# Aligning both halves of a warped path from its two corners in one Trainium2 kernel

## The reference, cut

```python
D = sqrt(max(aa + bb - 2 * xn @ ctx.T, 0))        # 128 x 128 distances of a batch
R[i, j] = D[i, j] + min(R[i-1, j], R[i, j-1], R[i-1, j-1])
# walk back from (127, 127) to (0, 0): the smallest of diagonal, up, left (the first at a tie)
expanded[j] += small[i]   for every (i, j) on the path
x = x + tanh(g_xattn[3]) * expanded
```

## Time and profile before

| | |
|---|---|
| median of 3 runs | 1556.9 us (1552.32, 1556.9, 1558.84) |
| the profiled execution | 1551.98 us, its span 1550.2 us |
| busy in the span | PE 1349.5 us, DVE 873.2, ACT 769.4, POOL 387.6 |
| the changed part | 1297.8 to 1470.3 us of the span |

### The profile page before, as it was taken

One profiled execution on the slowest core, in us unless ns is written; L12 is line 12 of the kernel. 1 busy time (PEld: TensorE's weight loads), 2 busy tenths in 40 slices (PEclk: granted clock), 3 DMA queues, 4 the chain that ended last, 5 costly groups with the idle time before them and its releaser, 6 DMA issues. The chain is left out here.

```text
span 1550.2 us, 31871 instructions
## 1 busy us (share of the span) xinstructions
PE 1349.5 (87%) x10589; PEld 1134.4 (73%) x10598; DVE 873.2 (56%) x2230; ACT 769.4 (50%) x1908; POOL 387.6 (25%) x544
## 2 busy tenths in 40 slices
PE   8999878889799999988999989999999998210588
PEld 5888646677689998767888869699999996210355
DVE  6988755656412222207777755623232274688887
ACT  5666474520354443537777753355555433340277
POOL 1000000012032221001222121356666544320141
PEclk9999999999899999999999997799999998655799
DMA  7200000772421117554434422022222354321001
GB/s 222 70 20 15 2 28 19 255 264 42 160 80 38 36 32 229 193 193 138 133 130 135 147 49 82 17 76 93 93 93 94 78 197 163 54 19 8 1 14 41
DMA packets 119253, 145.40 MB, mean 94 GB/s; under 512 B 39248, under 2 KB 96352, under 8 KB 119008
## 3 DMA queue, kind: packets, MB, share of 16 engines
q1 hardware_dynamic: 98048, 94.78, 19.4%
q0 software_dynamic: 10848, 27.88, 6.4%
q10 hardware_dynamic: 10240, 21.24, 3.9%
HBM read 105.22 MB, written 37.49 MB: 92 GB/s over the span
## 5 line engine op out<-in xcount | busy, mean ns | idle before, releaser
L3822 PEld LDWEIGHTS L2f_bank<-L2f_xT,L2f_w_tile 128*128 128x128 f32 x1264 | 154.1, 192 | 7.5 <-ACT L2f_xT L3895 3.5
L3822 PE MATMUL L2f_bank<-L2f_xT,L2f_w_tile 128*128 128x128 f32 x1264 | 154.8, 276 | 3.0 <-ACT L2f_xT L3895 3.0
L3959 DVE TENSOR_TENSOR L2f_hT<-L2f_gate_h,L2f_bank 128x256 f32<-128x256 f32 x79 | 33.3, 421 | 148.9 <-ACT L2f_gate_h L3902 148.9
L1188 ACT ACTIVATE L2x_probs<-L2x_shifted,L2x_top 128x128 f32<-128x128 f32 x256 | 99.0, 388 | 20.9 <-DVE L2x_top L1263 20.9
L1055 POOL TENSOR_TENSOR L2x_probs<-L2x_probs,L2x_inv_sum 128x512 f32<-128x512 f32 x32 | 33.3, 1039 | 264.1 <-DVE L2x_inv_sum L1272 264.1
L3745 POOL DMA_INDIRECT L2f_y_rows<-L2f_xn,L2f_put_row x79 | 78.0, 987 | 55.7 <-DVE L2f_xn L3975 52.1
L3889 ACT COPY L2f_w_tile<-L2f_w_up 128x1024 f32 x79 | 82.7, 1046 | 18.2 <-issue 18.2
L3737 POOL DMA_INDIRECT L2f_rows<-L2f_x_rows,L2f_take_row x79 | 76.8, 972 | 44.9 <-DVE L2f_take_row L3706 21.2
L3822 PEld LDWEIGHTS L1f_bank<-L1f_xT,L1f_w_tile 128*128 128x128 f32 x736 | 85.7, 192 | 2.8 <-ACT L1f_hT L924 1.7
L3822 PE MATMUL L1f_bank<-L1f_xT,L1f_w_tile 128*128 128x128 f32 x736 | 86.0, 275 | 1.5 <-ACT L1f_hT L924 1.5
L3839 PE MATMUL L1f_bank<-L1f_w_down,L1f_hT 128*128 x368 | 83.1, 379 | 0.0
(11 more groups left out here) (696 smaller groups left out, 3300.2 us busy)
## 6 DMA issues: line engine op xcount, KB each, us to landing
L1f_w_up<-in_L_ffn_w SPq DMA_DIRECT2D x16, 512.0 KB, 8.3
L1f_w_down<-in_L_ffn_w SPq DMA_DIRECT2D x16, 512.0 KB, 9.2
L2x_kT<-L2x_k_ahead SPq DMA_DIRECT2D x16, 512.0 KB, 4.6
L2x_v<-L2x_v_ahead SPq DMA_DIRECT2D x16, 512.0 KB, 3.3
L2f_got<-L2f_y_rows SPq DMA_DIRECT2D x16, 512.0 KB, 4.4
L2x_k_ahead<-L1f_w_tile ACTq DMA_DIRECT2D x11, 512.0 KB, 2.9
L2x_v_ahead<-L1f_w_tile ACTq DMA_DIRECT2D x11, 512.0 KB, 2.6
L2f_w_up<-in_L_ffn_gate_w SPq DMA_DIRECT2D x16, 256.0 KB, 3.7
```

The costliest lines, as they stand in the source:

```text
L1188: x = nc.scalar.activation(probs[c][:, i, :], shifted[c][:, i, :], ACT.Exp, scale=-1.0, bias=top[:, c, i:i + 1], accum_out=total[:, c, i:i ...
L3822: x = nc.tensor.matmul(products(j, m), w_tile[j][:, at:at + P], xT[j][:, k * P:(k + 1) * P], start=(k == 0), stop=(k == KT - 1))
L3959: nc.vector.tensor_tensor(hT[j][:, 0:F], gate_h[j][:, 0:F], bank[2 + j][:, F:2 * F], ALU.mult).then_inc(q["h"], 1)
```

## The change

The cost table is split at row 64. The first half is walked from the corner (0, 0), the second from (127, 127) with rows and columns reversed, both at once: 2 directions x 16 batches x 4 strips are 128 lanes, and the wave has 64 + 24 = 88 steps. NB falls from 8 to 4, so a block still has R = 16 rows. At the end the path's cell in the two middle rows is the minimum over the sum of the last rows of both halves (the "meeting"), and each half is walked back from there. For the reversal, TensorE multiplies with constants `both_ways` (identity and reversed identity, 256 columns) and `half_turned`, in plain products in place of transposes; the codes are put in order by one more product. The norm of x is computed from variance and rstd instead of from squares.

```diff
-    NB = 8
-    R = P // NB
+    H = P // 2
+    HB = 2 * B
+    NB = 4
+    R = H // NB
-    STEPS = P + (NQ - 1) * LEAD
+    STEPS = H + (NQ - 1) * LEAD
-    LANES = NQ * B
+    LANES = NQ * HB
...
-            eng.dma_start(dist3[q * B:(q + 1) * B, 1:CW, first:first + P], dist_dram[:, q * C:(q + 1) * C, :]
-                          ).then_inc(s[f"placed{q}"], 16)
+            for h in range(2):
+                at = q * HB + h * B
+                eng.dma_start(dist3[at:at + B, 1:CW, first:first + H],
+                              dist_dram[:, q * C:(q + 1) * C, h * H:(h + 1) * H]).then_inc(s[f"placed{q}"], 16)
...
-                sp.dma_start(low3[B:LANES, land, 0:1], cost3[0:LANES - B, edge, C:CW],
+                sp.dma_start(low3[HB:LANES, land, 0:1], cost3[0:LANES - HB, edge, C:CW],
...
+            nc.gpsimd.memset(both_ways[:, :, :], 0.0).then_inc(s["turned"], 1)
+            nc.gpsimd.memset(half_turned[:, :], 0.0).then_inc(s["turned"], 1)
...
-            def squares(b):
-                act.wait_ge(s["xn"], b + 1)
-                after(act, s["x_norm"], b)
-                nc.scalar.activation(x_sq[:, :], xn[b % 3][:, :], ACT.Square, accum_out=cols(x_norm, b, 1)
-                                     ).then_inc(s["x_norm"], 1)
+            def back_half(b):
+                act.wait_ge(s["dots"], b + 1)
+                act.wait_ge(s["x_norm_back"], 2)
+                after(act, s["dist"], b - 1)
+                nc.scalar.activation(sq_dist[b % 2][:, H:P], bank[4 + b % 2][:, H:P], ACT.Relu,
+                                     bias=x_norm[:, 1, b:b + 1]).then_inc(s["sq_back"], 1)
...
             def root(b):
+                back_half(b)
+                act.wait_ge(s["sq_back"], b + 1)
                 act.wait_ge(s["sq_dist"], b + 1)
...
-                    t = nc.tensor.transpose(bank[b % 2][:, k * P:(k + 1) * P], xn[b % 3][:, k * P:(k + 1) * P],
-                                            core.ident[:, :])
+                    t = nc.tensor.matmul(bank[b % 2][:, k * D:(k + 1) * D], xn[b % 3][:, k * P:(k + 1) * P],
+                                         both_ways[:, :, :].rearrange("p h c -> p (h c)"), start=True, stop=True)
...
-                    t = nc.tensor.transpose(bank[2 + b % 2][:, k * P:(k + 1) * P], ctx_all[:, b, k * P:(k + 1) * P],
-                                            core.ident[:, :])
+                    t = nc.tensor.matmul(bank[2 + b % 2][:, k * P:(k + 1) * P], ctx_all[:, b, k * P:(k + 1) * P],
+                                         half_turned[:, :], start=True, stop=True)
...
-                for k in range(KT):
-                    t = nc.tensor.matmul(dst, xT[b % 2][:, k * P:(k + 1) * P], ctx_neg2[b % 3][:, k * P:(k + 1) * P],
-                                         start=False, stop=(k == KT - 1))
+                for h in range(2):
+                    for k in range(KT):
+                        t = nc.tensor.matmul(dst[:, h * H:(h + 1) * H], xT[b % 2][:, k, h, :],
+                                             ctx_neg2[b % 3][:, k * P + h * H:k * P + (h + 1) * H],
+                                             start=False, stop=(h == 1 and k == KT - 1))
...
-            stay_warm(core, bank[7], 3)
+            stay_warm(core, bank[7], 2)
...
             pe.wait_ge(weights.sems["T_out"], 12)
+            pe.wait_ge(s["swap"], 2)
+            pe.wait_ge(c["blocks"], 16 * (NB * NQ + 1))
+            nc.tensor.matmul(bank[6][:, 0:HB], costs3[0:HB, R, 1:W], swap[:, :], start=True, stop=True
+                             ).then_inc(c["met"], 1)
...
+            dve.wait_ge(c["met"], 1)
+            nc.vector.tensor_copy(last_row[:, :], bank[6][:, 0:HB]).then_inc(c["met"], 1)
...
+            for d in range(2):
+                last = nc.vector.tensor_tensor(step_cost[:, d, :], costs3[0:HB, R, 1:W], other[:, d:d + P], ALU.add)
+            link(last)
...
+            link(nc.vector.tensor_reduce(best, step_cost[:, :, :], AX.XY, ALU.min))
+            link(nc.vector.scalar_tensor_tensor(step_cost[:, :, :], step_cost[:, :, :], best, preferred[:, :, :],
+                                                ALU.is_equal, ALU.mult))
+            link(nc.vector.tensor_reduce(chosen, step_cost[:, :, :], AX.XY, ALU.max))
...
+            nc.vector.tensor_copy(placed[:, :], bank[7][:, B:3 * B]).then_inc(c["placed_out"], 1)
```

More of the change, by code:

```diff
@@ L2699, in warped_alignment @@
         part = lambda at, n, k: [scratch[:, at + j * n:at + (j + 1) * n] for j in range(k)]
-        xn, xT, ctx_neg2 = part(0, D, 3), part(3 * D, D, 2), part(5 * D, D, 3)
+        xn, ctx_neg2 = part(0, D, 3), part(5 * D, D, 3)
+        xT = [t.rearrange("p (k h c) -> p k h c", k=KT, h=2) for t in part(8 * D + 2 * D + 3 * P, 2 * D, 2)]
         ctx_sq, ctx_sum = part(8 * D, D, 2), part(10 * D, P, 3)
-        x_sq = sb("x_sq", [P, D])
-        x_norm = sb("x_norm", [P, B])
+        x_norm = sb("x_norm", [P, 2, B])
+        both_ways = sb("both_ways", [P, 2, P])
+        half_turned = sb("half_turned", [P, P])
+        swap = sb("swap", [HB, HB])
         sq_dist = [sb(f"sq_dist{j}", [P, P]) for j in range(2)]
@@ L2712, in warped_alignment @@
             "quarter", "cleared", "xn", "xT", "xT_out", "ctxT", "ctx_neg2", "ctx_sq", "ctx_sum", "x_norm", "dots",
-            "sq_dist", "dist", "low", "row"] + [f"placed{q}" for q in range(NQ)] + [f"hand{i}" for i in range(HANDS)])
+            "sq_dist", "sq_back", "dist", "low", "row", "turned", "x_norm_back", "swap"] + [f"placed{q}" for q in range(NQ)] + [f"hand{i}" for i in range(HANDS)])
         c = core.sems_in("L3c", ["blocks", "step", "iota", "leave", "gathered", "enter", "entry", "ways", "turn", "unit",
-                                 "codes", "placed", "bounds", "signs", "mark", "out", "updated"])
+                                 "met", "codes", "placed", "placed_out", "ordered", "bounds", "signs", "mark", "out", "updated"])
         load_of = [i for i, n in enumerate(LOADS) for _ in range(n)]
@@ L2745, in warped_alignment @@
         inward = sb("inward", [P, P], BF16)
-        entry16 = sb("entry16", [B, NB])
-        spread = sb("spread", [B, NB, B])
-        of_block = sb("of_block", [P, NB])
+        entry16 = sb("entry16", [HB, NB])
+        spread = sb("spread", [HB, NB, HB])
+        of_block = sb("of_block", [P, 2, NB])
+        first_half = sb("first_half", [P, 4])
+        forward = sb("forward", [HB, 4])
+        other = sb("other", [HB, W])
+        step_cost = sb("step_cost", [HB, 2, P])
+        preferred = sb("preferred", [HB, 2, P])
+        meeting = sb("meeting", [HB, 4])
+        last_row = sb("last_row", [P, HB])
         of_batch = sb("of_batch", [P, B])
@@ L2869, in _ @@
             finish_norm_scalar(core, act, s, temps)
-            squares(0)
             take_xT(0)
@@ L2873, in _ @@
                 if b + 1 < B:
-                    squares(b + 1)
                     take_xT(b + 1)
@@ L2960, in _ @@
             pe.wait_ge(c["enter"], 1)
-            nc.tensor.matmul(bank[7][:, 0:1], spread[:, :, :].rearrange("b k c -> b (k c)"), core.ones[0:B, 0:1],
+            nc.tensor.matmul(bank[7][:, 0:1], spread[:, :, :].rearrange("b k c -> b (k c)"), core.ones[0:HB, 0:1],
                              start=True, stop=True).then_inc(c["entry"], 1)
@@ new lines, in _ @@
+            link(last)
+            link(nc.vector.tensor_scalar(preferred[:, 1, :], preferred[:, 1, :], 1.0, None, ALU.add))
+            dve.wait_ge(c["met"], 3)
+            link(nc.vector.tensor_copy(other[:, 0:P], bank[6][0:HB, P:2 * P]))
+            for d in range(2):
+                last = nc.vector.tensor_tensor(step_cost[:, d, :], costs3[0:HB, R, 1:W], other[:, d:d + P], ALU.add)
+            link(last)
+            best, chosen, diagonal = meeting[:, 0:1], meeting[:, 1:2], meeting[:, 2:3]
```

120 lines of the change are left out of this document (86 added, 34 removed).

## The result

In the same series of runs, twenty of each, the kernel before took 1554.76 us (median) and the changed one 1559.34 us. The ratio is 1.0038, with a 95% interval from 1.0026 to 1.0049: 4 to 8 us slower, inside the 0.5% that the prediction put ahead as "no change". By the medians it is +4.6 us, by the ratio +5.9; forecast was +5.6, and a time of 1562.5.

What follows compares the result with a forecast made beforehand. Each stage has its own limit: TensorE for distances, VectorE for wave and walk back. Terms 15.1+0.4+1.7+1.0-12.3-1.5+1.2 = +5.6 us on the median 1556.9 gave 1562.5 us; range 1552 to 1570.

Steps and rivals of the forecast that it cites:

- Distance stage: TensorE's distance products: more passes make a batch 2.42 us instead of 1.10; the stage's end moves by +15.1 us.
- narrow passes are cheap: Rival for the distance product: a pass of 64 columns costs half, saving 7.0 us, -1.4 in all, 1555.5 us; chance 0.12.
- The hand from ScalarE to VectorE: End of the last distance batch: one more half-width instruction and a semaphore lengthen it by +0.4 us.
- Read-back: Distances coming back in eight transfers of 256 B packets instead of four of 512 B: +1.7 us, between 0 and +3.4.
- First edge: First edge transfer of the wave queues on SP's ring behind the read-back; VectorE waits at step 9, 0 to 4, +1.0 us.
- Lanes are free: Wave: going from 64 to 128 lanes adds nothing to a step of 0.490 us.
- A scan longer than 0.23 us: Wave: a scan instruction above this time was listed as a sign that the forecast is wrong.
- Wave, ternary work, meeting: Wave to walk back: 64 fewer steps save 31.4 us, but 13.9 us go waiting for ternary weights; -12.3 us net.
- Joins and order of the marks: After the meeting: four of seven joins between blocks go, -1.5 us; ordering the marks costs +1.2 us.
- Signs: Marking stage: signs with a per-lane scale cost nothing, as ScalarE has 5.6 us to spare, 0.17 for each of 32.
- The norms: Distance stage: the norms cost nothing; 16 squares leave ScalarE, four small VectorE steps join during TensorE's warm-up.

Runs made afterwards that it cites:

- run 5: Kernel before with the distance product in four calls of 64 columns instead of two of 128; distance end +5.9 us, a batch 1.51 us instead of 1.11.
- Run 6: Kernel before with all TensorE distance work as in the changed one, identity twice instead of a reversal; 1566.55 us, ratio 1.0067, distance end +15.6 us.
- Run 8: Kernel before with each read-back transfer split in two of 64 columns, packets of 256 B; 5.42 us from issue to first step against 5.47.
- run 10: Changed kernel with reversal as transposes, scales before step 16, and SP's queue issuing only the first read-back transfer, ScalarE's the other three; 1540.14 us, ratio 0.9927.
- Run 1: Changed kernel with VectorE's two weight-scale instructions before step 16 of the wave instead of step 80; 1547.82 us, ratio 0.995 to the kernel before.
- run 2: Kernel before with VectorE's two weight-scale instructions before step 16 instead of step 80, as control; 1552.59 us, ratio 0.9988.
- run 11: Kernel before with x's norm taken from the norm's constants, no squares on ScalarE; distance end 26.7 us instead of 29.3, 2.0 us inside the part.
- run 7: Kernel before with the wave's tiles over 128 lanes, upper half zero, transfers as they were; wave 77.2 us instead of 74.5.
- run 3: Changed kernel with the reversing products as transposes, one pass instead of two; 1555.12 us, ratio 1.0002 to the kernel before.

## Why the prediction was right, point by point

Each term was measured inside the part, changed kernel against before. In short: the path was right, the longer distance stage and the ternary weights that wait for step 80, and with them the two large terms; of the small ones, read-back and first edge had the wrong reason, and the dearer steps and the signs were put at nothing.

- **Distance stage, forecast +15.1: +15.4.** The batch of 2.42 us came out, and so did the reading of the earlier trace rows that a narrow pass costs as much as a wide one: 0.105 in run 5. So the rival "narrow passes are cheap" is out. The some 60 cycles up to 64 columns in the Trainium skill, "TensorE: Matmul & The Clock Gate", section "Back-to-back issue gap", are the gap of a product alone, and the section itself says that at small widths this counts too little in a stream of weight loads and products. The trace agrees with that: 0.105 us for 64 columns, with a load each. Run 6 shows that passes alone explain the stage.
- **The hand from ScalarE to VectorE, forecast +0.4:** +0.4.
- **Read-back, forecast +1.7, the middle between bytes (0) and count (+3.4): +1.4.** The size was right by luck: other profiles of the two read-backs put it anywhere from +0.2 to +1.5. The middle stood for no cause. Run 8 shows that the count alone costs nothing; in the changed kernel, whose packets took 51 ns, the last transfer lands 3.1 us later than before. The Trainium skill, "DMA: Bandwidth & Descriptors", section "Specifications", puts the smallest transfer at line rate at 512 B. This case doesn't settle it: in run 8 packets of 256 B came in at the time of those of 512, in the changed kernel they did not. What makes the difference, four runs did not find. That no transfer in the rows had smaller pieces was a slip: the earlier trace rows has packets of 4 B.
- **First edge, forecast +1.0: +1.6** (1.6 us at step 9, where the kernel before has no wait). It does stand behind the read-back, but not by way of SP's ring: with one transfer ahead of it there, run 10 still has 1.3 us. In every profile it lands right behind the read-back's last transfer, so this term and the one above seem to have one cause.
- **"Lanes are free": wrong by a little.** Doubling them adds 8 and 11 ns to the two instructions of a step, some 1.7 us over the 88 steps. "A scan longer than 0.23 us" was one of the signs of being wrong, and the scan takes 0.239; the term is small, so the sum held all the same. I had two rows of different widths and read from them a rule that they only bound.
- **Wave, ternary work, meeting, forecast -12.3: -9.7 from the wave's first step to the walk back**, or -11.3 of forecast with the edge's wait in it. The mechanism was right in each part: ScalarE's chain 20.5 us as before, meeting 5.1 against 5.2, and the wait found where it was put. Of the 1.6 us missing 1.5 are the dearer steps ahead of step 80 (79 x 0.019) and 0.6 the longer wait for the first edge; two waits of 0.25 us, which the kernel before has among those steps and this one once, give some of it back. Run 1 took the wait away and 13.75 us came back, where the text had 13.9; run 2 shows that in the kernel before the same line was worth nothing.
- **Joins and order of the marks, forecast -0.3: -0.5** up to the bounds.
- **Signs, forecast 0: +0.4** from the bounds on. An ACTIVATE with a per-lane scale takes 0.50 and 0.48 us instead of 0.41 and 0.39. Two of them per batch are 0.78 us from start to start. But ScalarE is busy 12.6 of 16.3 us, so 3.7 of the 5.6 us to spare are left, and the stage's clock also differs (0.81 against 0.89). That the signs make the 0.4 is not shown.
- **The norms, forecast 0:** at most 0.2 us in the changed kernel, whose distance end is 44.7 against 44.9 in run 6, which keeps the squares. Alone in the kernel before they were worth some 2 us in the one profile of run 11, where the clock did not fall.

The sum was +5.6 forecast, +7.4 in the pair of profiles, +4.6 to +5.9 over twenty runs. The difference of 1.5 to 2.8 us between profile and runs is of the size of what the distance end alone moves between executions with other clocks at their start (27.3 to 29.3 us in run 7 and the kernel before, whose distance stages are the same). That the whole times agree with the forecast to within a microsecond is therefore partly luck; that it is a small loss and not a gain of some 8 us follows from the path that the prediction had right.

## What to carry to other kernels

Shortening the longest stage moves everything that was timed by it. Here a side chain hung on a step number ("step 80") that had been in the middle of a wave and came to lie at its end. When a loop is cut short, look for the work that is released from inside it, and give it an earlier step, if its inputs exist by then: worth 13.75 us here, and nothing before the cut.

In these traces an f32 product with a constant 0/1 matrix takes two passes, the transpose form with the same constant takes one (2.42 and 1.70 us a batch), and the result was right with a permutation in place of the identity. And cutting a product into narrower calls did not cut its time: with 128-wide weights a pass of 64 columns cost what one of 128 did, 0.105 us.

A mean between two bounds can come out right and stand for no cause. Only runs that take away one cause at a time tell whether the middle was knowledge.

## What the runs showed of the hardware

- Doubling the lanes from 64 to 128 cost 184 to 192 ns for a minimum over 32 columns and 228 to 239 ns for a scan over 33 (run 7).
- A read-back in packets of 256 B (run 8) took no longer than one of the same bytes in packets of 512 B (5.42 and 5.47 us to the first step), while equal packets of 256 B in the changed kernel cost 51 ns instead of 34 (open).
- A small transfer that is issued while a large one is under way landed 0.2 to 1.2 us behind the large one's last piece, in all fourteen profiles, also where it was alone on its queue (run 10: 4.5 us instead of the usual 1.8).
- After a pause of PE of 1.91 us the granted clock fell from 1.00 to 0.5 for about 3 us although PE was full again. The same shows in run 3 (pause 2.08 us, 0.61 from 1316 to 1320); after the 1.46 us of run 11 the clock stayed. The changed kernel pauses 0.57 us at most and ran at 0.99 over its 39.5 us, so its longer work had less waste than that of before (38.9 of 39.5 us busy against 21.3 of 24.0).
- The start of the last layer's attention differs by 13.7 us between the fourteen profiles, with the same text ahead of it, and by 8.0 among the eight kernels built on the one before. A pair of profiles can only be compared from a common event, not from the start of the span.
